# Two attention blocks in fp32: a shorter layer norm chain, a plain last projection, and five steps put elsewhere in the queues

## The reference

```
x = x + L0(group_norm(x))
x = x + L1(group_norm(x))
L0: channel LN -> 1x1 to q,k,v -> depthwise 3x3 -> softmax(q), softmax(k) over positions
    -> linear attention, 8 heads of 16 -> silu -> 1x1 -> channel LN
L1: 1x1 to 384 -> depthwise 5x5, grouped 1x1 (second set of q,k,v)
    -> relu linear attention over both sets, 32 heads of 8 (v padded by ones, divided)
    -> 1x1 from 256 channels to 128 -> batch norm
```

## Time and profile before

| | |
|---|---|
| median of 3 runs | 340.18 us (338.6 to 341.18) |
| profiled execution | 342.08 us, span 340.3 us |
| PE busy | 263.5 us (77%) |
| DVE busy | 209.4 us (62%) |
| ACT busy | 160.7 us (47%) |
| POOL busy | 129.0 us (38%) |
| mean granted TensorE clock | 0.960 |

### The profile page before, as it was taken

How to read it: one execution, slowest core, us unless ns; L and a number is a source line. 1 busy time by engine, 2 the same in 40 slices (tenths; PEclk the granted TensorE clock), 3 DMA queues, 4 the chain that set the end, 5 groups by cost and what they waited for, 6 DMA issues and landing times.

```text
span 340.3 us, 13545 instructions
## 1 busy us (share of the span) xinstructions
PE 263.5 (77%) x5779; PEld 201.5 (59%) x5779; DVE 209.4 (62%) x680; ACT 160.7 (47%) x390; POOL 129.0 (38%) x343
## 2 busy tenths in 40 slices
PE   0348987678868698885989498886898989879993
PEld 0235756446546477664667466665677777667871
DVE  3775977328875456888696645553432333569994
ACT  0558753079734366864563314433333236226653
POOL 8156563019565427765432202212132232143200
PEclk9999998969997999998799879999999999999999
DMA  8630296841001400000026530804200000000112
GB/s 237 97 84 3 45 224 135 194 119 37 4 2 27 95 3 3 1 2 0 4 44 148 118 71 2 187 3 119 71 4 4 6 4 4 5 2 33 65 62 94
DMA packets 15756, 20.08 MB, mean 59 GB/s; under 512 B 4160, under 2 KB 9280, under 8 KB 15680
## 3 DMA queue, kind: packets, MB, share of 16 engines
q1 hardware_dynamic: 12128, 18.03, 22.2%
q10 hardware_dynamic: 3568, 1.18, 1.9%
HBM read 4.33 MB, written 2.30 MB: 19 GB/s over the span
## 4 chain that ended last, share of the span: by engine, by line
PE 50%; DVE 22%; POOL 9%; issue 8%; ACT 5%; ACTq 2%; DMA 2%; SPq 0%; DVEq 0%; POOLq 0%
PE bank L1108 46%; PE bank L1104 4%; DVE cin L859 3%; POOL ring_v L449 2%; DMA xin<-in_x_dram 2%; ACT rings L516 2%; ACTq L298 1%; DVE xres L1076 1%; DVE den L1000 1%; DVE proj_parts L1051 1%; DVE rings L1002 1%; DVE ctxm L984 1%; POOL cpos L431 1%; DVE ctxm L982 1%; DVE proj_parts L1083 1%
## 5 line engine op out<-in xcount | busy, mean ns | idle before, releaser
L1108 PE MATMUL bank<-cin,tband 64*32 64x240 f32 (+2 forms) x3072 | 87.4, 374 | 16.6 <-ACT tband L577 10.3
L1108 PEld LDWEIGHTS bank<-cin,tband 64*32 64x32 f32 x3072 | 66.0, 108 | 36.9 <-issue 14.3
L907 DVE STREAM_TRANSPOSE cpos<-bank 128x256 f32<-128x256 f32 x96 | 37.1, 427 | 56.2 <-PE bank L1108 56.2
L1104 PE MATMUL bank<-ident,rings 128*128 128x128 f32 x192 | 34.0, 307 | 34.9 <-ACT rings L516 12.2
L577 ACT ACTIVATE tband<-tband,row_edge 128x96 f32<-128x96 f32 (+1 forms) x96 | 32.3, 395 | 41.1 <-POOL tband L413 40.9
L1104 PEld LDWEIGHTS bank<-ident,rings 128*128 128x128 f32 x192 | 22.5, 153 | 45.9 <-issue 19.8
L859 DVE STREAM_TRANSPOSE cin<-bank 128x768 f32<-128x768 f32 x32 | 31.0, 977 | 20.9 <-PE bank L1108 20.9
L449 POOL TENSOR_SCALAR ring_v<-cpos,mask_b 128x512 f32<-128x512 f32 x30 | 20.9, 709 | 36.7 <-PE bank L1108 21.2
L413 POOL TENSOR_TENSOR tband<-taps,pw 128x320 f32<-128x320 f32 x24 | 17.7, 737 | 40.7 <-PE bank L1108 40.7
L516 ACT ACTIVATE rings<-bank,ln_b,ln_s 128x128 f32<-128x128 f32 x64 | 24.1, 460 | 14.4 <-POOL ln_b L401 14.2
L449 POOL TENSOR_SCALAR ring_v<-rings,mask_b 128x512 f32<-128x512 f32 x16 | 10.9, 692 | 49.9 <-ACT rings L655 49.9
(11 more groups left out here) (133 smaller groups left out, 452.1 us busy)
## 6 DMA issues: line engine op xcount, KB each, us to landing
cin<-cin SPq DMA_DIRECT2D x48, 192.0 KB, 4.2
cin<-cin SPq DMA_DIRECT2D x40, 64.0 KB, 2.0
xin<-in_x_dram SPq DMA_DIRECT2D x4, 512.0 KB, 6.2
out_dram<-rings SPq DMA_DIRECT2D x8, 256.0 KB, 2.2
taps<-tap_rows SPq DMA_DIRECT2D x16, 60.0 KB
taps<-tap_rows SPq DMA_DIRECT2D x16, 36.0 KB
cin<-cin ACTq DMA_DIRECT2D x8, 64.0 KB, 2.2
rings<-in_L_conv_w_qkv_dram ACTq DMA_DIRECT2D x1, 192.0 KB, 6.7
```

The source lines that it names most:

```text
L907: last = v.transpose(cpos[n % NS // TS][:, :, :, g * CG:(g + 1) * CG], bank[2 * (n % 4) + q][:, 0:B * HH])
L1104: last = t_.transpose(tile(dst, xl), src(xl), ident[:, :])
L1108: return t_.matmul(dst, stationary, moving, start=start, stop=stop, skip_group_check=True)
```

## The change

Six things are changed at once:

- `layernorm` on GpSimd has 12 operations; the two that read the moments (variance plus eps, minus mean) are VectorE's now, behind `bn_aggr`.
- The last projection takes plain fp32 operands: two products per pair. ACT adds the batch norm's bias to the residual once, before the tail; `y` adds product and residual straight into the output's natural order; the output is stored image by image.
- `q_scale` comes behind band 16, 18, 20, 22 (before: 13, 15, 17, 19), `q_sum` behind set 9, 11, 13, 15 (before: 11, 13, 15, 17).
- In the first front end `fold_batchnorm` moves from step 7 to step 2, `small_masks` from step 4 to step 2, the statistics of images 8 to 11 from before the loop into step 0; VectorE scales the second image of the first pair; TensorE does the products of pairs 0 and 6 ahead of the back transpose of that step.
- The last group statistics are taken at step 13 in place of 14.
- ACT's `half_out` goes ahead of `front1`.

```diff
-GN1 = ((0, 2, 8), (2, 5, 11), (5, 8, 14))
+GN1 = ((0, 2, 8), (2, 5, 11), (5, 8, 13))
...
             def layernorm(n):
-                w, y, t, less = (lnt[:, k, :] for k in range(4))
-                scale, mean, var = ln_s[:, n % 2, :], lmv[:, n % 2, :, 0], lmv[:, n % 2, :, 1]
+                y, t = lnt[:, 0, :], lnt[:, 1, :]
+                scale, w, less = ln_s[:, n % 2, :], lnw[:, n % 2, 0, :], lnw[:, n % 2, 1, :]
                 pool.wait_ge(s_lmv, n + 1)
                 if n >= 1:
                     pool.wait_ge(s_ln, n)
-                g.tensor_scalar(less, mean, -1.0, 1.0, ALU.mult, ALU.mult)
-                link(g.tensor_scalar(w, var, EPS, 1.0, ALU.add, ALU.mult))
...
-                m = n - 13
+                m = n - 16
                 if m >= 0 and m % 2 == 0 and m // 2 < NQ:
                     q_scale(m // 2)
...
             def xg(i):
-                for b in range(2):
+                for b in range(2 if i else 1):
...
+                if 0 <= n - 4 < PAIRS:
+                    half_out(n - 4)
                 if 0 <= n < PAIRS:
                     front1(n)
                 if n == PAIRS - 1:
                     last_odd_quads(1)
-                if 0 <= n - 4 < PAIRS:
-                    half_out(n - 4)
...
+            for i in range(PAIRS):
+                last = a.activation(xres[:, i, :], xres[:, i, :], ACT.Identity, bias=bn_bias[:, :])
+            last.then_inc(s_xb, 1)
             def half1_out(i):
                 act.wait_ge(s_ot, PAIRS + i + 1)
-                a.copy(proj_parts[:, i % 2, 1, 0, :], bank[7][:, :]).then_inc(s_half, 1)
...
+                a.copy(half1[:, i % 2, :], bank[7][:, :]).then_inc(s_half, 1)
...
                 for xl in range(XL):
-                    last = v.bn_aggr(lmv[:, n % 2, xl, :], lstats[:, xl, :])
-                last.then_inc(s_lmv, 1)
+                    last = v.bn_aggr(lmv[:, xl, :], lstats[:, xl, :])
+                link(last)
+                v.tensor_scalar(lnw[:, n % 2, 0, :], lmv[:, :, 1], EPS, None, ALU.add)
+                v.tensor_scalar(lnw[:, n % 2, 1, :], lmv[:, :, 0], -1.0, None, ALU.mult).then_inc(s_lmv, 1)
...
             gn_scale(0, 0, B // 2, bank[7])
+            dve.wait_ge(s_gn, 1)
+            v.tensor_scalar(image3(ring_a[:, 0, :], 1), natural(xin[:, NPOS:2 * NPOS]), gn_s[:, 1:2], gn_b[:, 1:2],
+                            ALU.mult, ALU.add).then_inc(s_xg0, 1)
             tap_rows()
-            x_stats(B // 2, 3 * B // 4)
...
                 if step == 0:
-                    link(x_stats(3 * B // 4, B))
+                    link(x_stats(B // 2, B))
...
                 if step == 2:
                     gn_scale(1, B // 2, B // 2, bank[7])
-                if step == 4:
                     dve.wait_ge(s_ident, 1)
                     small_masks()
-                if step == PAIRS - 1:
                     fold_batchnorm()
...
-                m = n - 11
+                m = n - 9
                 if m >= 0 and m % 2 == 0 and m // 2 < NQ:
                     q_sum(m // 2)
...
             def y(i):
                 dve.wait_ge(s_fin, i + 1)
+                if i >= 2:
+                    dve.wait_ge(s_out[i % 2], 32 * (i // 2))
                 for b in range(2):
-                    r = image(xres[:, i, :], b)
-                    last = v.scalar_tensor_tensor(
-                        out=r, in0=bank[2][:, b * NPOS:(b + 1) * NPOS].rearrange("p (n y) -> p n y", y=HH),
-                        scalar=bn_bias[:, :], in1=r, op0=ALU.add, op1=ALU.add)
+                    v.tensor_tensor(natural(ring_b[:, i % 2, b * NPOS:(b + 1) * NPOS]),
+                                    bank[2][:, b * NPOS:(b + 1) * NPOS].rearrange("p (l h y) -> p l h y", l=XL, h=XH),
+                                    image3(xres[:, i, :], b), ALU.add).then_inc(s_y, 1)
...
+                if step - 3 in (0, PAIRS - 2):
+                    front_units(step - 3)
                 if 0 <= step - 2 < PAIRS:
+                    back(step - 2)
+                if 0 <= step - 3 < PAIRS and step - 3 not in (0, PAIRS - 2):
+                    front_units(step - 3)
...
-                for q_w, q_in in ((0, 0), (0, 1), (1, 0)):
-                    last = product(bank[2][:, :], w_parts[:, half, q_w, :], proj_parts[:, i % 2, half, q_in, :],
-                                   start=(half, q_w, q_in) == (0, 0, 0), stop=half == 1 and q_w == 1)
+                last = product(bank[2][:, :], wpt[:, half, :], half1[:, i % 2, :] if half else half0[:, i, :],
+                               start=half == 0, stop=half == 1)
```

More of the change, by code:

```diff
@@ L341, in _ @@
             for i in range(PAIRS):
-                sp.wait_ge(s_yp, i + 1)
-                sp.dma_start(out[2 * i:2 * i + 2].rearrange("b c h w -> c b (h w)"),
-                             ring_b[:, i % 2, :].rearrange("p (b n) -> p b n", b=2)).then_inc(s_out[i % 2], 16)
+                for b in range(2):
+                    sp.wait_ge(s_y, 2 * i + b + 1)
+                    sp.dma_start(out[2 * i + b].rearrange("c h w -> c (h w)"),
+                                 ring_b[:, i % 2, b * NPOS:(b + 1) * NPOS]).then_inc(s_out[i % 2], 16)
             for n in range(2):
-                sp.wait_ge(s_out[n], 16 * PAIRS // 2)
+                sp.wait_ge(s_out[n], 16 * PAIRS)
         @block.gpsimd
@@ L1137, in _, with back, front_units @@
             pe.wait_ge(s_wte, 1)
+            def back(i):
+                pe.wait_ge(s_nrm, i + 1)
+                if i >= 1:
+                    pe.wait_ge(s_xn, i)
+                transposes(bank[2], lambda xl: tile(ring_b[:, i % 2, :], xl)).then_inc(s_nrm_t, 1)
+            def front_units(i):
+                pe.wait_ge(s_xn, i + 1)
+                for n in range(2):
+                    if i >= 1:
+                        pe.wait_ge(s_cin, 2 * (i - 1) + n + 1)
+                    if i == 0 and n == 1:
+                        pe.wait_ge(s_gn, 2)
+                    units(n, ring_c[:, i % 2, :], w0t, 4).then_inc(s_qkv, 1)
             for step in range(PAIRS + 3):
@@ L1141, in _ @@
                     pe.wait_ge(s_xg, i + 1)
+                    if i == 0:
+                        pe.wait_ge(s_xg0, 1)
                     if i >= 3:
@@ L1144, in _ @@
                     transposes(bank[X_BANKS[i % 3]], lambda xl: tile(ring_a[:, i % 2, :], xl)).then_inc(s_xgt, 1)
+                if step - 3 in (0, PAIRS - 2):
+                    front_units(step - 3)
                 if 0 <= step - 2 < PAIRS:
-                    i = step - 2
-                    pe.wait_ge(s_nrm, i + 1)
-                    if i >= 1:
-                        pe.wait_ge(s_xn, i)
-                    transposes(bank[2], lambda xl: tile(ring_b[:, i % 2, :], xl)).then_inc(s_nrm_t, 1)
-                if 0 <= step - 3 < PAIRS:
-                    i = step - 3
-                    pe.wait_ge(s_xn, i + 1)
-                    for n in range(2):
-                        if i >= 1:
-                            pe.wait_ge(s_cin, 2 * (i - 1) + n + 1)
-                        if i == 0 and n == 1:
-                            pe.wait_ge(s_gn, 2)
-                        units(n, ring_c[:, i % 2, :], w0t, 4).then_inc(s_qkv, 1)
+                    back(step - 2)
+                if 0 <= step - 3 < PAIRS and step - 3 not in (0, PAIRS - 2):
+                    front_units(step - 3)
                 if step == 1:
```

64 lines of the change are left out of this document (15 added, 49 removed).

## The result

The changed kernel takes 326.37 us (median of 4 runs, 325.31 to 326.66) where the one before took 340.68 in the same comparison (338.6 to 342.27, 4 runs): ratio 0.957, 95% interval 0.953 to 0.961. The traced execution took 326.22 us with a span of 324.5, against 342.08 and 340.3. The forecast was 321.0, with 313 to 331 around it.

What follows compares the result with a forecast made beforehand. The prediction held that no engine bounds the whole program, with TensorE holding half of the chain of waits. Its six terms summed to −19.2 us, taking the median from 340.2 to 321.0, with 313 to 331 holding 8 in 10.

Steps and rivals of the forecast that it cites:

- q's order, -7.8: First convolution: q scaling three bands later, sum two sets earlier; 7.8 us less, 6.1 of it waits, the rest slow clock.
- The sign that I had set: First convolution, sets 12 to 23: TensorE without a wait over 0.5 us for edge scalings, GpSimd's q-sum wait zero.
- rival A: First front end, attention and convolution: VectorE's added work gets in the way, total 328.3 us; chance 0.14.
- Front end, -2.3: First front end: fold and small masks earlier, last conversion ends at 62.0 in place of 64.5; 2.3 us less.
- Layer norm, -1.2: First attention: two GpSimd operations per pair go, VectorE gets two, 4.95 us a step; 1.2 us less.
- 0.3 less on four steps: First attention: each of four steps taken as 0.3 us shorter, at 4.95 us a step.
- Statistics at step 13, -1.7: Second front end: the 4.34 us wait goes, a new one of 3.3 comes, half clock loss taken; 1.7 us less.
- rival B: Second front end: new waits keep their place, earlier statistics return nothing, half_out gives 1.5 us; total 327.9 us; chance 0.12.
- half_out ahead, -4.4: Second front end: transposes at steps 5 to 7 no longer wait for ACT, 3.4 us, plus 1.0 at step 8.
- the fourth term: Second front end, step 8: 1.0 us gained, limited by the last odd quads, about 2.2 us in flight.
- Projection, -1.8: Tail: two plain fp32 products replace six, pairs stay at 4.25 us, the end comes 1.8 us earlier.
- Rival C: Tail: VectorE's strided output sum, at 3 us each, makes the kernel slower, 350.6 us; chance 0.05 with like mishaps.

Runs made afterwards that it cites:

- u_half: The changed kernel with ACT's half_out put back behind front1: 326.28 us, ratio 0.960 to the kernel before.
- warm: The changed kernel with transposes that nobody reads put into four waits of TensorE: 319.78 us, ratio 0.934 to the kernel before.

## Why the forecast held, and where its terms were off

The forecast was 5.4 us too low, inside its range. Against the changes of the two traces (span 15.8 us shorter, 19.2 summed), term by term:

1. **q's order, -7.8: the mechanism right, the waits somewhat smaller.** The traces give 6.0 and 7.25 us (on the changed kernel and on the kernel before), undoing it gives 8.2. It is 5.0 to 5.3 us of waits and 0.8 to 3.2 of clock loss; I had 6.1 and 1.7. The sign that I had set, no wait over 0.5 us for edges from set 12 on, did not quite come: set 12 itself still waits 1.10 us (88.00), where it waited 0.88 before. The 6.1 had counted that wait as gone; with the edit alone on the kernel before 1.3 us of such waits stayed as well. From set 13 on there is none. No part of rival A came here: VectorE's sums held up nothing.

2. **Front end, -2.3: the size right by luck, the path not.** The start came 2.8 us earlier. Nine kernels with this front end start at 67.65 on average where the two with the old one have 70.25, 2.6 earlier; without loss it is 66.5 (65.8 to 67.3) and 68.5, 2.0 earlier. But the last conversion ended at 60.59, where I had 62.0 (and 64.46 before), and the convolution did not follow it: 3.9 us earlier there, 2.8 here. The step that failed is the path, "the last conversion ends at 62.0 in place of 64.5" taken for the start itself. Before, the start waited for ACT's edges, which stand behind ACT's issue of the last transfers; now the wait ends with a transfer in seven of the nine traces, and with the edges in two. The transfers crowd ahead of that wait, which begins at 62.15:

```profile
56.00:62.00 6.00, 4.13 (x76) 3.17 (x75) 2.48 (x3) 0.58 (x1) 0.00 (x0) 1.00 1.06 212
```
```profile
56.00:62.00 6.00, 5.67 (x100) 5.00 (x104) 3.01 (x4) 0.00 (x0) 0.00 (x0) 0.72 0.59 135
```

The first is the changed kernel, the second the one before; the last column but one is the share of the DMA engines: 1.06 against 0.59. With such a second bound close behind, the fold's place and pair 6's place, each undone, cost nothing that the totals show. The two were not undone together, and which edit brings the 2.0 to 2.6 us was not tried.

3. **Layer norm, -1.2: the term that was most off for its size.** It gave 0.4 us over the three steps that it can shorten; of the whole stage without loss the pairs of traces show 0.7 (47.18 and 46.50) and 0.9 (47.39 and 46.50), but kernels with the same layer norm differ by as much (46.5 to 47.4). GpSimd could run at 4.83 us a pair (maskings at 124.31 and 129.14), as the arithmetic wanted; VectorE then has the longest list. From 128.27 to past 135.48 its rows follow on each other without one wait:

```profile
128.27 0.73 DVE L947 SCALAR_TENSOR_TENSOR xres<-bank,vecs,xres 128x512 f32<-128x512 f32 x1
...
129.32 0.53 DVE L837 TENSOR_SCALAR lnw<-lmv 128x4 f32<-128x4 f32 x1
...
131.15 0.74 DVE L953 BATCH_NORM_STATS2 gstats<-xres 128x6 f32<-128x256 f32 x2
131.81 0.68 DVE L907 TENSOR_REDUCE kneg<-bank 128x2 f32<-128x512 f32 x1
132.49 0.89 DVE L825 BATCH_NORM_STATS2 lstats<-bank 128x6 f32<-128x128 f32 x4
133.29 0.73 DVE L947 SCALAR_TENSOR_TENSOR xres<-bank,vecs,xres 128x512 f32<-128x512 f32 x1
133.94 0.37 DVE L835 BATCH_NORM_AGGREGATE lmv<-lstats 128x2 f32<-128x6 f32 x4
134.35 0.37 DVE L837 TENSOR_SCALAR lnw<-lmv 128x4 f32<-128x4 f32 x1
134.63 0.16 DVE L838 TENSOR_SCALAR lnw<-lmv 128x4 f32<-128x4 f32 x1
```

The first new operation begins on GpSimd's masking twice: it takes 0.53 at 129.32 (masking from 129.14), 0.37 at 134.35 (masking from 134.00), and 0.17 elsewhere; the second is never held. One round of the list, 128.27 to 133.29, is 5.02 us. Without the 0.36 of the hold it is 4.66, so the 4.7 of the prediction and its 4.95 with a hold were nearly right for this step. The step that failed is "0.3 less on four steps": the next two rounds are 5.17 and 5.24 us, since VectorE's list has the group statistics in them as well (0.38 us at 136.79, four small operations from 141.64), and the gain shrinks from 0.22 to nothing. The Trainium skill, "SBUF — State Buffer", section "Who interferes with whom", says that where VectorE works in a two-port mode, it and GpSimd lock each other out: the one that comes second is blocked for the other's whole instruction. The trace agrees: from 129.32 the operation ends at 129.85, with the first of the two masking instructions of 0.69 us (from 129.14). The prediction's reading of that rule, both new operations held and the term 0, came out near in size and wrong in how: one of them was held, in two steps.

4. **Statistics at step 13, -1.7: the waits right, the clock by luck.** The new wait is 3.36 us (3.3 forecast). Counted from the start of the stage, the product behind it came 2.5 us later (2.3 forecast) and the third one 1.9 earlier (2.1). The fourth came 5.1 earlier, 1.0 of it by part 5, so this pair of traces gives about 4 us for the part, near the 4.1 that the prediction had before it took something off for a low clock behind the new wait. That low clock did not come in this trace, but it did in seven of the ten traced kernels with the statistics at step 13, with 1.6 to 3.2 us of loss (u_half, for one):

```profile
167.58 0.36 PE L1074 MATMUL bank<-gmv,mean 128*128 128x6 f32 x2 [3.35 <-DVE gmv L799]
```
```profile
169.00:170.00 1.00, 1.00 (x8) 0.50 1.01 205
```

Undoing the part costs 1.9 without loss, so rival B, a new wait with no return, is out. The prediction's own working does not end at its -1.7: 4.1 less the whole 2.7 is 1.4, less half of it 2.75.

5. **half_out ahead, -4.4: the mechanism of the three steps right (3.0 us for 3.4), the fourth term mis-sized.** Steps of 7.37 for 7.3 forecast, 8.38 with the order undone. The term for step 8, 1.0, was worked out with 2.2 us of flight for the last transfers. ACT's last issue ends at 214.50 + 1.90 = 216.40 and the convolution, which waits for a transfer, starts at 219.69: 3.3 us. (In warm it started 2.9 us behind the issue, so the flight differs from trace to trace.)

```profile
213.95 0.52 ACTq L295 DMA_DIRECT2D cin<-cin  x1
214.50 1.90 ACTq L295 DMA_DIRECT2D cin<-cin  x3
```

The order undone cost 3.0 us without loss in the changed kernel and 3.3 in the warm one, of which the three steps are 3.0: so step 8 gives 0 or 0.3. Behind its 2.13 us wait this trace had the low clock (1.6 us). Both undone, 4 and 5 make 4.4 us without loss where I had 6.1.

6. **Projection, -1.8: right**, 1.6 by the tails: 43.74 and 43.73 us with fp32r (before, and put back), 43.75 in the warm kernel, 42.14 changed. A plain product of 512 columns (two records) takes 0.86 to 0.96 us start to start, as the estimate of 0.95 had it, the two of a pair 1.82, and TensorE, now without a pause in the full pairs, bounds them. Such a pair took 4.37 us and not 4.25; the four of them lose 0.5 by that, and the end gains it back. Rival C's sum with steps of 64 bytes is at busy 0.52 us each and a mean of 598 ns, where the one before, with steps of 8, was at 0.43 and 483:

```profile
L1051 DVE TENSOR_TENSOR rings<-bank,xres 128x256 f32<-128x256 f32 x14 | 7.3, 598 | 0.6 <-PE bank L1074 0.3
```

The Trainium skill, "SBUF — State Buffer", section "Door 1: The DMA port swizzle", has a penalty for every access in a new 16-byte line. The sum got a fifth to a quarter dearer and not the double of the prediction's estimate, and here the measurement decides. How much of it is the step is not shown, since the operation changed with it (one scalar operand less).

By stages, the 3.4 us between 19.2 and 15.8 are: 0.5 more than forecast up to the first convolution, 1.8 less in it (6.0 for 7.8), 1.8 less in the attention (0.6 lost where 1.2 were to be gained, with 2.7 us of clock loss in place of 1.4), 0.9 more in the second front end (7.0 for 6.1), 1.0 less in the second convolution, 0.2 less in the tail. So the total is near the forecast by several misses of either sign: of the 7.0 in the second front end 2.5 are clock, which another execution need not give.

## What to carry to other kernels

Walk the queues instruction by instruction, as part 1 did: a wait that a queue holds for an engine which could go on is the surest gain. Of each such gain ask what ends last next, transfers too (here a share of 1.06 of the DMA engines ahead of the wait); a conversion that ends sooner only moves their wait. Judge an edit of 1 to 3 us by its stage in the trace with the clock loss taken out, since the totals of six undone edits lay between 1.5 us below and 2.3 above the changed kernel, in no order of their worth; and where TensorE waits and its clock falls behind, try unread transposes: in four places together they took the ratio from 0.957 to 0.934, or 0.943 over all runs, 5 to 8 us. Where it does not wait they only add their own time, 2.3 us for twenty. And walk more than one round of a loop: VectorE's list was longer in the next two rounds than in the one that the forecast was worked out from (part 3).

## What was not expected of the chip

**The low clock wanders.** Fourteen traced kernels, before and after among them, lose between 3.4 and 12.4 us to it; the places differ from one to the next, in stages that are the same code. Much of it lies behind a wait of TensorE of 2 to 6 us, but not every such wait is followed by it: the one at step 13, of 3.0 to 3.4 us in ten traced kernels, was followed by it in seven and not in three. The two levels are 1.00 and 0.50 (2.4 and 1.2 GHz). Between runs of one kernel it goes with the largest differences seen: warm's runs at a mean clock of 1.000 took 316.0 and 317.8 us, those at 0.979 321.8.

**Gaps between blocks of products.** The second convolution took 58.4 to 61.7 us without loss, in kernels that have the same code there. The timeline of TensorE in the kernel before and in the one with q's edits alone, both at clock 1.00:

```profile
262.80 3.42 PE L1108 MATMUL bank<-cin,tband 64*32 64x224 f32 x127 [0.52 <-issue]
266.64 3.57 PE L1108 MATMUL bank<-cin,tband 64*32 64x224 f32 x127 [0.42 <-issue]
270.47 3.44 PE L1108 MATMUL bank<-cin,tband 64*32 64x240 f32 x127 [0.27 <-issue]
274.61 3.43 PE L1108 MATMUL bank<-cin,tband 64*32 64x256 f32 x128 [0.70 <-issue]
```
```profile
253.14 11.53 PE L1108 MATMUL bank<-cin,tband 64*32 64x256 f32 x409
265.37 3.43 PE L1108 MATMUL bank<-cin,tband 64*32 64x256 f32 x128 [0.70 <-issue]
```

After 127 or 128 products, in places after 254, there is a pause of 0.15 to 0.70 us that nothing in the profile releases, ten times and 4.7 us in all in the first kernel, six times and 2.5 us in the second, where 409 products ran without one: 2.2 us of difference by this alone. The Trainium skill, "Runtime: NRT & Kernel Launch", section "Instruction fetch mechanics", says that an engine's instructions are fetched in blocks of 256 and that the cost is mostly hidden. 128 products with their weight loads are 256 instructions, so the spacing of most pauses agrees. No run tested that fetching is the cause; if it is, it was hidden in some of the blocks and not in others.
